# A routed ViT block on one core: the experts' one-hot rows made in three parts in another chunk, and two bias additions put ahead of the slice's lower half

## What is computed

```
scores = xf @ gate_w.T
scores = (jnp.tanh(scores) + 1.0) * 0.5
vals, idx = jax.lax.top_k(scores.T, k)
kept_w = vals.T
flat_idx = idx.T.reshape(-1)
y = xf[flat_idx].reshape(k, n, d)
y = _layernorm(y, ln_gamma, ln_beta)
h = jnp.einsum('knd,nfd->knf', y, fc1s) + b1s
h = jax.nn.gelu(h, approximate=True)
o = jnp.einsum('knf,ndf->knd', h, fc2s) + b2s
o = o * kept_w[:, :, None]
out = xf.at[flat_idx].add(o.reshape(k * n, d))
```

## Time and profile before

| | |
|---|---|
| median of 3 runs | 795.19 us (793.22 to 795.29) |
| the profiled execution | 794.65 us, of which 792.8 us from the first to the last instruction |
| busy over the span | PE 700.8 us (88%), DVE 548.8 (69%), POOL 494.8 (62%), ACT 457.7 (58%) |
| granted TensorE clock | mean 0.943 of full speed |

### The profile page before, as it was taken

One profiled execution on the slowest core, in us unless ns is written; L12 is line 12 of the kernel. 1 busy time (PEld: TensorE's weight loads), 2 busy tenths in 40 slices (PEclk: granted clock), 3 DMA queues, 4 the chain that ended last, 5 costly groups with the idle time before them and its releaser, 6 DMA issues.

```text
span 792.8 us, 15802 instructions
## 1 busy us (share of the span) xinstructions
PE 700.8 (88%) x4630; PEld 635.1 (80%) x4630; DVE 548.8 (69%) x1821; ACT 457.7 (58%) x1063; POOL 494.8 (62%) x724
## 2 busy tenths in 40 slices
PE   6987999999999963527999999999999999999994
PEld 3976788888888743416998998989989999899993
DVE  3765789998999867988785675766846757634431
ACT  1003587777777768604466566665665566656551
POOL 0257699999999755334258476484684764846523
PEclk9989999999999985557999999999999999999997
DMA  9900022221222227212035234343352433432222
GB/s 261 300 15 1 4 82 79 79 70 66 76 79 80 81 99 145 97 42 74 15 54 152 44 76 108 50 126 67 54 149 41 91 92 52 128 69 45 39 27 27
DMA packets 63564, 64.15 MB, mean 81 GB/s; under 512 B 14032, under 2 KB 57104, under 8 KB 63376
## 3 DMA queue, kind: packets, MB, share of 16 engines
q1 hardware_dynamic: 50576, 46.33, 19.3%
q0 software_dynamic: 12800, 17.12, 13.2%
q10 hardware_dynamic: 128, 0.00, 0.0%
HBM read 37.90 MB, written 25.53 MB: 80 GB/s over the span
## 4 chain that ended last, share of the span: by engine, by line
PE 35%; DVE 10%; issue 6%; POOL 5%; ACT 4%; DMA 2%; POOLq 0%; DVEq 0%; ACTq 0%; SPq 0%
PE bank L1031 16%; PE bank L1045 14%; PE bank L1020 2%; PE bank L1057 2%; POOL out L591 1%; POOL w2l L550 1%; DVE ge L1436 1%; DMA raw<-in_fc1T 1%; DVE yl L1586 1%; ACT bank L766 1%; POOL yg L569 1%; DVE ohu L1538 1%; PE bank L1010 1%; DVE jk L1563 1%; ACT hh L769 1%
## 5 line engine op out<-in xcount | busy, mean ns | idle before, releaser
L591 POOL DMA_INDIRECT out<-ob,sidx x72 | 114.0, 1583 | 159.6 <-ACT ob L782 137.0
L1593 DVE TENSOR_TENSOR hl<-bank,hh 128x384 fp32r<-128x384 f32 (+1 forms) x192 | 97.5, 513 | 138.8 <-ACT hh L769 134.7
L766 ACT ACTIVATE bank<-bank,b1s 128x384 f32<-128x384 f32 (+1 forms) x192 | 99.4, 518 | 137.7 <-PE bank L1031 131.9
L1031 PE MATMUL bank<-yh,w1h 128*128 128x384 f32 (+1 forms) x384 | 133.3, 347 | 8.9 <-DVE hl L1593 5.7
L1031 PE MATMUL bank<-yh,w1l 128*128 128x384 f32 (+1 forms) x384 | 124.0, 323 | 0.0
L1031 PE MATMUL bank<-yl,w1h 128*128 128x384 f32 (+1 forms) x384 | 123.7, 322 | 0.0
L1045 PE MATMUL bank<-w2l,hh 128*128 128x256 f32 x384 | 108.0, 281 | 0.0
L1045 PE MATMUL bank<-w2h,hh 128*128 128x256 f32 x384 | 108.0, 281 | 0.0
L1045 PE MATMUL bank<-w2h,hl 128*128 128x256 f32 x384 | 107.9, 281 | 0.0
L569 POOL DMA_INDIRECT yg<-rows,idx x72 | 72.6, 1008 | 44.2 <-issue 39.1
L769 ACT ACTIVATE hh<-bank 128x384 fp32r<-128x384 f32 (+1 forms) x192 | 87.8, 457 | 6.1
(11 more groups left out here) (249 smaller groups left out, 1795.0 us busy)
## 6 DMA issues: line engine op xcount, KB each, us to landing
BIG<-in_x SPq DMA_DIRECT2D x4, 2048.0 KB, 17.0
out<-Bs SPq DMA_DIRECT2D x32, 256.0 KB, 2.2
rows<-Yp SPq DMA_DIRECT2D x32, 256.0 KB, 2.4
raw<-in_fc1T SPq DMA_DIRECT2D x16, 512.0 KB
raw<-in_fc2T SPq DMA_DIRECT2D x16, 512.0 KB
yg<-rows,idx POOLq DMA_INDIRECT x72, 2.9
out<-ob,sidx POOLq DMA_INDIRECT x72, 3.8
gwb<-in_gate_w SPq DMA_DIRECT2D x1, 1024.0 KB, 7.5
```

What stands on the lines that cost most here:

```text
L591: g.indirect_dma_start(out=out_rows, out_offset=tok(ap=sidx[job.eh][0:m, t:t + 1], axis=0), in_=ob[t % 3][0:m, :], in_offset=None, compute ...
L766: A.activation(h[:, 0:cur.w], h[:, 0:cur.w], ACT.Gelu_apprx_tanh, bias=b1s[:, bass.ds(cur.e, 1), f]).then_inc(s["hact"], 1)
L1031: last = T.matmul(Lb[ring(cur, f)][:, 0:cur.w], w1s[cur.eh][i][:, d, f * P:(f + 1) * P], yT[cur.p][k][:, d, 0:cur.w], start=(n == 0), stop ...
L1593: v.tensor_tensor(hT[cur.p][1][:, f, 0:cur.w], Lb[ring(cur, f)][:, 0:cur.w], hT[cur.p][0][:, f, 0:cur.w], ALU.subtract).then_inc(s["hlo"], 1)
```

## The change

The table for expert q + 2 is no longer made behind the last tile in chunk 2, but in chunk 0 of expert q (q = 1 to 5), in three parts: columns 0 to 383 in slice 1, 384 to 767 in slice 4, 768 to 1027 in slice 6, each behind that slice's `low_hidden`. The tables of experts 1 and 2 are made as before. A table that the loop made for a ninth expert, which nothing reads, is gone: eight whole tables become two whole ones and five in parts. `tail_bias` stands ahead of the slice's `low_hidden` where it stood behind it.

```diff
+        OH_AT = (1, 4, 6)
...
-            def one_hot(job, c0=0, c1=KTOK, begun="ohu", done="ohd"):
+            def one_hot(job, c0=0, c1=KTOK, begun="ohu", done="ohd", n=None):
...
-                dve.wait_ge(s[begun], job.q + 1)
+                dve.wait_ge(s[begun], job.q + 1 if n is None else n)
...
+            def one_hot_part(job, part):
+
+
+                c0, c1 = ((0, 3 * P), (3 * P, 6 * P), (6 * P, KTOK))[part]
+                one_hot(job, c0, c1, "ohu", "ohd" if part == 2 else "oh_part", job.q * 3 - 5 + part)
...
-                if t == 8 and job.q_next:
+                if t == 8 and isinstance(job.q, int) and job.q < 2:
                     one_hot(Job(job.el, job.eh * 3 + 3))
...
             def emit(prev, cur, nxt, tiles):
+                far = cur.plus(2) if cur and cur.c == 0 and not (isinstance(cur.q, int) and cur.q in (0, 6, 7)) else None
                 for f in SLICES:
+                    if prev and prev.c == 2 and f in OT_AT[0:2]:
+                        tail_bias(prev, OT_AT.index(f))
                     if cur:
                         low_hidden(cur, f)
-                    if prev and f in OT_AT:
-                        u = OT_AT.index(f)
-                        if prev.c < 2:
-                            with_bias(prev, prev.t0 + u)
-                        elif u < 2:
-                            tail_bias(prev, u)
+                    if prev and prev.c < 2 and f in OT_AT:
+                        with_bias(prev, prev.t0 + OT_AT.index(f))
+                    if far and f in OH_AT:
+                        one_hot_part(far, OH_AT.index(f))
                     if nxt and f == TURN_AT:
                         scaled(nxt)
```

More of the change, by code:

```diff
@@ L250, in build_program @@
             st1_b st1 tug teg base yp tab base_st0 base_st1 yp_st0 yp_st1
-            gt_c gt_t gt_v vt_st vsp_t vsp levels v_set thr0 thr1 tc by_v0 by_v1 by_a0 by_a1 pass0 pass1 next0 next1 try0 try1 tlo0 tlo1 tf0 tf1 tk_c tk_mm oh_begun oh_first
+            gt_c gt_t gt_v vt_st vsp_t vsp levels v_set thr0 thr1 tc by_v0 by_v1 by_a0 by_a1 pass0 pass1 next0 next1 try0 try1 tlo0 tlo1 tf0 tf1 tk_c tk_mm oh_begun oh_first oh_part
             ohd smm smc ixc ixd wld0 wld1 bld0 bld1 whi wlo0 wlo1 hhi hlo yhi yr gat00 gat01 gat02 gat10 gat11 gat12 yt_t yt hmm hact om oadd omul omt oev obk scat0 scat1 scat2 idc""".split()
@@ L321, in __init__, with plus @@
                 self.w = sum(SLOTS[self.t0:self.t1])
+            def plus(self, experts):
+                return Job(self.el, self.k + 3 * experts)
         def place_bank(job, t):
```

## The result

The changed kernel took 809.84 us (median of 4 runs, 809.52 to 810.49) against 794.48 us before (4 runs, 793.22 to 795.29): 1.0188 times as long, with an interval of 1.0176 to 1.0201. The forecast was 803.0 us and its range ended at 806.5. The profiled execution of the changed kernel took 809.85 us, 808.0 us of it the span, against 792.8 us before.

A forecast was written before the change was run, and what follows sets the result against it. The prediction took the chain POOL, load, ACT, DVE at each change of expert as the bound. Terms -1.7 + 1.0 + 8.9 = +8.2 us gave 803.4 on the median, stated as 803.0 us; range 793.3 to 806.5 us.

The forecast's parts named there:

- The chain of the change of expert: Chunk 0: POOL's second half of w2l, load, ACT, then DVE's hl and yl end last; PE's waits lie inside it.
- the 8.7 us: PE's waits for hl (5.7) and oT (3.0): none counted as gain; rival that they bound: 786.5 us, chance 0.11.
- The relief of the scatters: Chunk 2: POOL's scatter, no longer lengthened by ohu, gets 0.28 us shorter, six times: -1.7 us.
- the five lines of the sum: Slice 4, experts 1 to 5: table part waits for POOL's w1l, delaying slice 5's hl and yl: 8.9 us.
- The ties of experts 1 and 5: Slice 4: DVE and POOL nearly ready together; counted as held; if both cost nothing, the sum would be 4.9 us.
- Part 0: Slice 1: its oh may delay POOL's second half of w2l, 0.2 us at five experts: +1.0 us.
- The clock falls: Rival: PE's five stands lower its clock, 1.5 us each, 7.5 in all, giving 810.5 us; chance 0.05.

The follow-up runs named there:

- the bias alone: Kernel before the change, with only the bias additions of chunk 2 put ahead of the slice's hl: 794.43 us, ratio 1.0003.
- part 1 out of the way: Changed kernel with the three table parts in slices 1, 6 and 7 instead of 1, 4 and 6: 793.80 us, ratio 0.9996.
- The kernel with PE kept busy: Changed kernel plus twelve unused products on PE ahead of the wait for yl in experts 1 to 5: 803.51 us, ratio 1.0101.
- the kernel with the parts alone: Changed kernel with the bias additions put back behind hl, leaving only the one-hot parts: 806.50 us, ratio 1.0153.
- the one with the narrow part: Changed kernel with parts of 640, 128 and 260 columns, so slice 4's is 128 wide instead of 384: 808.79 us, ratio 1.0177.

## Why the prediction was wrong

**What held.** The chain of the change of expert is POOL, load, ACT, DVE, and what PE loses inside it is free. The waits of PE that the change removed, 7.4 of the 8.7 us in the earlier trace rows, bought nothing (the bias alone 1.0003; part 1 out of the way 0.9996). The relief of the scatters was -1.69 us, predicted -1.7. `ohu` in slice 4 was held behind `w1l` in all five experts (2.18 to 2.77 us each) and ended 0.22 to 0.24 us behind it. Taking the kernel with part 1 late as the one without the hold, the holds were 2.04, 1.96, 1.40, 1.38 and 1.92 us, 8.7 in all, where the five lines of the sum gave 1.95, 1.88, 1.56, 1.45 and 2.04, 8.9. The ties of experts 1 and 5 went to POOL, and not by coming first: `ohu` was issued 0.15 and 0.03 us ahead of `w1l` (in expert 2 by 0.15 as well), and still waited for it. Had DVE won them it would have gone the same way, as far as one case tells: in the changed kernel with the scatter moved `ohu` was first in expert 1, and then `oh` was held, 3.12 us. That is the rule of the Trainium skill (SBUF — State Buffer, Who interferes with whom) that a VectorE instruction with two SBUF inputs contends with a GpSimd instruction that reads SBUF; the traces agree, with 3.12 and 3.22 us for 0.62, and with 4.19 us for the whole table's.

**A term that was off.** Part 0 was put at +1.0 us, for POOL held by `oh`. It was nothing, the other way round: in all five experts part 0 was held by POOL (`oh` in experts 1, 2 and 4, `ohu` in 3 and 5), and nobody waited. By terms the sum should have read -1.7 + 0 + 8.7 = +7.0, which is what the timelines of chunk 0 show.

**The step that failed** is the rival "The clock falls", with "the same stretch had been stop-and-go for long, and these waits stand in a busy one" as its reason against it, and the chance of 0.05. It happened behind four of the five stands and cost 7.6 us; its price in the prediction was 7.5, and its 810.5 us is near the measured 809.84. That the two agree so closely is partly luck: the price was five times 1.5 us, and it came as 1.5, 1.7, 0.0, 1.65 and 2.65. Two things were wrong in the weighing. First, the stand was put only at "over 2 us", and it was 2.64 to 3.48 us. The prediction had shown that the waits for `hl` and `oT` would be handed to `yl`, and had not added them: in expert 2 the 0.42 us of before, the 1.73 that chunk 0 grew by, and the 0.69 for `hl` and 0.50 for `oT` that PE had waited there before make 3.34 us, and it stood for 3.48. Second, a busy stretch was taken for safety, and it is no protection: in expert 2 PE was busy 3.93 of the 4 us up to 484.00, a microsecond ahead of its stand, at a granted clock of 1.00, and at work without a gap behind it. The kernel with PE kept busy shows the cause, since the hold is in it and the fall is not. That the range left this case out was the same error again, because the only argument against it was a likeness, with no row in which PE stood for 2 us and more and kept its clock.

**What stays open.** In the changed kernel the clock did not fall behind the stand of 2.64 us in expert 3. It fell behind 2.30 us in the kernel with the parts alone, behind 2.40 us in the one with the narrow part, and behind 0.71 and 1.43 us in the one with `w1l` moved, so the length of the stand alone does not decide it; no row here tells what does. The 0.6 us ahead of expert 1, where the changed parts have not yet run, are not explained; the same point lies between 412.8 and 415.4 us in the traces of all the kernels here. Nor is PE's stall on its own "issue" explained, 4.9 us in the profiled execution of the kernel with the twelve products, for which only the place is known.

## What to carry to other kernels

Before moving DVE work into a gap, look for what POOL does in that gap. Here an instruction with two operands in SBUF, or a plain `tensor_scalar` from SBUF to SBUF, waited for the whole of POOL's 2.4 us subtraction, at 128 columns as at 1028; its slot should lie behind the step that others wait for. When a wait is only taken from one place and the start behind it stays, add up what all the stands at that place come to: here 13 of the 14 stands of PE for `yl` of 2.3 us and more were followed by a stretch 1.5 to 2.9 us longer, about as much again as the hold that made them, and a shorter one was too. And shorten the chain that ends last at its head: one scatter put behind `w2l` was worth 12 us with the table out of its way, and cost 12 us with the table in it.

## What the runs showed of the hardware

- A DVE instruction that is issued while a gather runs on POOL may wait for the POOL subtraction that comes behind the gather as well: `oh` issued at 474.92, in the gather of 474.28 to 475.28, ended at 478.14, 0.42 us behind the end of `w2l`. POOL started `w2l` 0.03 us behind the gather, ahead of the DVE instruction that had waited longer. The `ohu` issued 0.09 us after the gather's start ran in its usual 0.41 us.
- Being issued ahead of POOL's subtraction did not help while a gather ran: `ohu` issued at 483.64 waited for the `w1l` that started at 483.79.
- Behind the release a blocked instruction needed its own time less some 0.2 us: 0.22 us of 0.41 for an `ohu` of 384 columns, 0.42 of 0.62 for such an `oh`, 1.09 of 1.29 for the whole `oh`.
- The granted clock fell behind single stands of 2.30 to 3.76 us, once behind stands of 0.71 and 1.43 us, and stayed behind one of 2.64 us. Where it fell it was back at 1.00 some 4 us after the start in expert 2 of the changed kernel; in expert 5 it was 0.50 over the first 4 us, 0.76 over the next and 1.00 only then.
